# Attention layer: transposes of the score maxima moved from TensorE to VectorE, statistics and tail rearranged

## The reference

```python
B, T, D, H = 8, 512, 256, 16                    # head width 16
xn = layer_norm(x, norm_w, norm_b)
q = (xn @ q_w + q_b).reshape(B, T, H, 16)
k = (xn @ k_w + k_b).reshape(B, T, H, 16)
att = einsum('bnhl,bmhl->bnmh', q, k) + (1 - mask) * -1e6
att = softmax(att, axis=2)                      # over the keys m
v = ((xn @ v_w + v_b) * mask).reshape(B, T, H, 16)
y = einsum('bnmh,bmhl->bnhl', att, v).reshape(B, T, D)
e = silu(emb) @ emb_w + emb_b                   # emb is (8, 512)
scale, shift = split(e, 2)
h = layer_norm(y, sb_norm_w, sb_norm_b) * (1 + scale) + shift
out = x + silu(h) @ out_w + out_b
```

## Time and profile before

| | us |
|---|---|
| three runs | 513.33, 514.04, 513.12 |
| median | 513.33 |
| profiled execution | 512.97 |
| its span, first to last instruction | 511.2 |
| mean granted clock of TensorE | 1.00 |
| busy: TensorE, VectorE, ScalarE, POOL | 498.2, 408.1, 355.1, 232.3 |

### The profile page before, as it was taken

One profiled execution on the slowest core, in us unless ns is written; L12 is line 12 of the kernel. 1 busy time (PEld: TensorE's weight loads), 2 busy tenths in 40 slices (PEclk: granted clock), 3 DMA queues, 4 the chain that ended last, 5 costly groups with the idle time before them and its releaser, 6 DMA issues.

```text
span 511.2 us, 10072 instructions
## 1 busy us (share of the span) xinstructions
PE 498.2 (97%) x2829; PEld 188.8 (37%) x2829; DVE 408.1 (80%) x656; ACT 355.1 (69%) x647; POOL 232.3 (45%) x279
## 2 busy tenths in 40 slices
PE   8999999999999999999999999999999999999887
PEld 3433333343334333333334333343434343332225
DVE  7898778796888879797897978888788877879614
ACT  2336777678767778676867788677777778667872
POOL 5764333554354534635434643536346444333701
PEclk9999999999999999999999999999999999999999
DMA  5445452343423543334433443235433342234002
GB/s 153 134 138 158 121 167 93 105 126 111 126 74 109 151 144 105 100 90 144 123 89 120 146 132 108 76 100 154 135 104 115 92 142 82 87 110 144 0 2 83
DMA packets 54586, 57.42 MB, mean 112 GB/s; under 512 B 12424, under 2 KB 41736, under 8 KB 54560
## 3 DMA queue, kind: packets, MB, share of 16 engines
q1 hardware_dynamic: 51808, 54.74, 36.4%
q10 hardware_dynamic: 2752, 2.37, 1.6%
HBM read 35.82 MB, written 21.00 MB: 111 GB/s over the span
## 4 chain that ended last, share of the span: by engine, by line
PE 85%; DVE 7%; issue 3%; ACT 2%; POOL 1%; DMA 1%; POOLq 0%; ACTq 0%; DVEq 0%
PE pv_ps L625 24%; PE st_ps L609 22%; PE mx_ps L557 13%; PE job_ps L693 10%; PE job_ps L702 5%; DVE negmax L1092 4%; PE job_ps L714 3%; PE mx_ps L742 2%; ACT probs L858 2%; PE mx_ps L589 2%; PE mx_ps L668 1%; PE mx_ps L750 1%; DVE x_stats L1096 1%; DMA k_rows<-qk_dram 1%; PE job_ps L519 0%
## 5 line engine op out<-in xcount | busy, mean ns | idle before, releaser
L1092 DVE TENSOR_REDUCE negmax<-mx_ps 128x2 f32<-128x1024 f32 x256 | 304.8, 1220 | 76.3 <-PE mx_ps L557 75.9
L858 ACT ACTIVATE probs<-st_ps 128x512 f32<-128x512 f32 x502 | 272.4, 596 | 110.3 <-PE st_ps L609 105.8
L609 PE MATMUL st_ps<-q_rows,k_rows 115*128 115x512 bf16 x498 | 154.2, 383 | 2.4 <-ACT probs L858 0.9
L625 PE MATMUL pv_ps<-probs,v_rows 128*32 128x512 f32 x1024 | 136.4, 605 | 0.6 <-ACT probs L858 0.6
L1369 POOL TENSOR_TENSOR qk_parts<-qk_rest,qk_parts 128x512 bf16<-128x512 f32 x31 | 35.9, 1159 | 132.2 <-DVE qk_parts L1170 131.4
L557 PE MATMUL mx_ps<-k_rows,q_rows 51*128 51x512 bf16 x512 | 79.8, 382 | 1.8 <-DMA k_rows<-qk_dram 0.7
L609 PEld LDWEIGHTS st_ps<-q_rows,k_rows 115*128 115x128 bf16 x498 | 38.9, 97 | 106.3 <-ACT probs L858 75.4
L1354 POOL TENSOR_TENSOR qk_parts<-qk_full,zero 128x512 bf16<-128x512 f32 x29 | 30.1, 1039 | 72.1 <-ACT qk_full L888 72.1
L693 PE MATMUL job_ps<-x_norm_t,w_qk 128*128 128x512 f32 x116 | 59.6, 594 | 0.0
L557 PEld LDWEIGHTS mx_ps<-k_rows,q_rows 51*128 51x128 bf16 x512 | 16.3, 94 | 107.0 <-DVE negmax L1092 51.6
L1360 POOL TENSOR_TENSOR qk_rest<-qk_full,qk_parts 128x512 f32<-128x512 f32 x31 | 35.8, 1156 | 3.5 <-ACT qk_parts L876 1.2
(11 more groups left out here) (151 smaller groups left out, 401.0 us busy)
## 6 DMA issues: line engine op xcount, KB each, us to landing
qk_dram<-qk_parts SPq DMA_DIRECT2D x128, 128.0 KB
q_rows<-qk_dram SPq DMA_DIRECT2D x124, 96.0 KB, 2.6
k_rows<-qk_dram SPq DMA_DIRECT2D x124, 96.0 KB, 2.6
x_in<-in_x SPq DMA_DIRECT2D x16, 256.0 KB, 3.0
x_res<-in_x SPq DMA_DIRECT2D x7, 512.0 KB, 4.6
out<-out_sb SPq DMA_DIRECT2D x14, 256.0 KB, 2.5
k_rows<-mask_dram SPq DMA_DIRECT2D x64, 6.0 KB
w_e<-in_L_cond_emb_w ACTq DMA_DIRECT2D x4, 256.0 KB, 3.3
```

Of the source, the lines that this page charges most:

```text
L609: pe.matmul(st_bank(b, t, h), k_rows[0:ROWS_ALL, g, h, c * P:(c + 1) * P], q_rows[0:ROWS_ALL, g, h, :], start=True, stop=True).then_inc(st ...
L625: mm = pe.matmul(pv_ps[VW * h:VW * (h + 1), :], v_rows[:, c, g * GH + h, :], probs[:, t % P_SLOTS, h, :], start=(c == 0), stop=(c == CH - ...
L858: act.activation(probs[:, t % P_SLOTS, h, :], st_bank(b, t, h), ACT.Exp).then_inc(exp_done, 1)
L1092: dve.tensor_reduce(by_pair[:, :, j, c], mx_ps[j][:, :, :], AXIS_X, ALU.max, negate=True).then_inc(max_done, 1)
```

## The change

The turn of a group's maxima runs on VectorE, as four transposes of 32x32 blocks from `negmax` (padded to 32 columns) into a new tile `neg_rows`, ahead of reduction 0; the split reads `neg_rows` and stands behind reduction 0. Three turns stay on TensorE with the old order of the split: (0,0), (1,0) and (3,7). For the other 29, TensorE no longer waits for the split. The statistics of x go from t = 11 to 15 to t = 7 and 8, and `load_x` on SyncE from behind `spread(b, 0, 1)` to ahead of it. In the tail the last turn of y, its copy, moments, root and norms go by halves, `late_out` stands behind the turn of y but for one matmul, and the warming matmuls go.

```diff
+BLOCK = 32
-X_STAT = {(11, 0): (0,), (11, 2): (1,), (12, 2): (2,), (13, 1): (3,), (15, 0): (4,)}
+X_STAT = {(7, 2): (0, 1, 2), (8, 0): (3,), (8, 2): (4,)}
-WARM_LAST = 6
+def turn_on_pe(b, step):
+    turn = turn_at(b, step)
+    return turn is not None and isinstance(turn[1], int) and turn in ((0, 0), (1, 0), (NG - 1, B - 1))
-        negmax = sb("negmax", [P, 2, GH * CH])
+        negmax = sb("negmax", [P, 2, BLOCK])
+        neg_rows = sb("neg_rows", [BLOCK, P])
 # TensorE
             def max_pair(b, t, j):
+                if j == 1 and turn_on_pe(b, t):
+                    pe.wait_ge(max_split, turn_at(b, t)[0] + 1)
-                if j == 1 and turn_at(b, t):
-                    turn, turn_b = turn_at(b, t)
-                    pe.wait_ge(max_split, NG * turn_b + turn + 1)
             def max_turn(b, t):
-                if not turn_at(b, t):
+                if not turn_at(b, t) or not turn_on_pe(b, t):
                     return
+            def late_out(i, c, features):
...
+            def last_yturn():
+                pe.wait_ge(h_ready, KD * (B - 1))
+                pe.wait_ge(y_ready, NG * B - 1)
+                late_out(0, 0, range(1))
+                pe.wait_ge(max_done, PAIRS * STEPS * B)
+                for half in range(2):
+                    pe.wait_ge(last_yt, half + 1)
+                    for c in range(2 * half, 2 * half + 2):
+                        mm = pe.transpose(last_ps[0][half][:, c * P:(c + 1) * P], y_t[:, c * P:(c + 1) * P], ident[:, :])
+                    mm.then_inc(last_y, 1)
+                late_out(0, 0, range(1, KD))
+                late_out(0, 1, range(KD)).then_inc(turned["outp"], 1)
+                late_out(1, 0, range(KD))
+                late_out(1, 1, range(KD)).then_inc(turned["outp"], 1)
             def last_rows():
-                keep_warm(st_ps[0], WARM_LAST)
...
-                    if not short(b, t):
-                        max_turn(b, t)
 # ScalarE
+                if isinstance(b, int) and (b, g) == (B - 1, NG - 1):
+                    for half in range(2):
+                        tok = slice(2 * P * half, 2 * P * (half + 1))
+                        act.copy(y_t[:, tok], pv_ps[:, tok]).then_inc(last_yt, 1)
+                    return
                 act.copy(y_t[:, :], pv_ps[:, :]).then_inc(yt_ready, 1)
 # VectorE
             dve.memset(warm_in[:, :].bitcast(F32), 0.0).then_inc(warm_ready, 1)
+            dve.memset(negmax[:, :, GH * CH:], 0.0).then_inc(pad_ready, 1)
+            def turn_max(b, t):
+                if not turn_at(b, t) or turn_on_pe(b, t):
+                    return
+                i, d = turn_at(b, t)
+                n = NG * d + i
+                if isinstance(d, int) and n == 2:
+                    dve.wait_ge(pad_ready, 1)
+                dve.wait_ge(max_done, PAIRS * CH * (n + 1))
+                dve.wait_ge(max_split, n)
+                for c in range(CH):
+                    dve.transpose(neg_rows[:, BLOCK * c:BLOCK * (c + 1)], negmax[BLOCK * c:BLOCK * (c + 1), i % 2, :]
+                                  ).then_inc(turned["cturn"], 1)
-            def split_max(b, t):
+            def split_max(b, t, place):
+                if not turn_at(b, t) or place != (0 if turn_on_pe(b, t) else 1):
+                    return
...
-                dve.tensor_copy(parts[0], ps).then_inc(split_chain, 1)
+                dve.tensor_copy(parts[0], rows).then_inc(split_chain, 1)
                 dve.wait_ge(split_chain, n + 1)
-                dve.tensor_tensor(parts[1], ps, parts[0], ALU.subtract).then_inc(max_split, 1)
+                dve.tensor_tensor(parts[1], rows, parts[0], ALU.subtract).then_inc(max_split, 1)
...
+            def last_half(half):
+                chunks = slice(2 * half, 2 * half + 2)
+                by_head = last_ps[0][half][:, :].rearrange("p (c h w) -> p c h w", h=GH, w=VW)[:, chunks]
+                dve.wait_ge(last_y, half + 1)
+                dve.reciprocal(y_recip[:, chunks, :], by_head[:, :, :, HD]).then_inc(recip_ready, 1)
...
             def last_rows():
+                last_half(0)
+                last_half(1)
                 dve.wait_ge(turned["hturn"], KD * (B - 1))
                 for half in range(2):
+                    last_norm_half(half)
+                    late_sum(half)
...
                     stats_at(b, t, 0)
-                    split_max(b, t)
+                    turn_max(b, t)
+                    split_max(b, t, 0)
                     max_pair(b, t, 0)
+                    split_max(b, t, 1)
                     late_job(b, t, 1)
                     stats_at(b, t, 1)
                     max_pair(b, t, 1)
 # POOL
             def last_norms():
                 for half in range(2):
+                    chunks, c = slice(2 * half, 2 * half + 2), 2 * half
+                    pool.wait_ge(y_stat_ready, B + half)
+                    pool.tensor_tensor(y_rstd[:, chunks], y_vareps[:, chunks], exponent[:, chunks], ALU.pow
+                                       ).then_inc(y_rstd_ready, 1)
+                    pool.wait_ge(y_rstd_ready, B + half)
                     pool.tensor_scalar(y_norm[:, c, :], y[:, c, :], y_negmean[:, c:c + 1], y_rstd[:, c:c + 1],
                                        ALU.add, ALU.mult).then_inc(last_norm[half], 1)
 # SyncE, body(b)
-                spread(b, 0, 1)
                 if exists(b + 2) and not (isinstance(b, int) and b == -1):
                     wait_apart(sp, maskp_ready, x_norm_ready, CH * (b + 2))
                     load_x(b + 2)
+                spread(b, 0, 1)
```

More of the change, by code:

```diff
@@ L562, in max_pair, with max_turn @@
                     keep_warm(pv_ps, WARM_MAX.get((step, j), 0))
+            def max_turn(b, t):
+                if not turn_at(b, t) or not turn_on_pe(b, t):
+                    return
+                i, d = turn_at(b, t)
+                pe.wait_ge(max_done, PAIRS * CH * (NG * d + i + 1))
+                pe.transpose(mx_ps[1][0:GH * CH, 0, 0:P], negmax[:, i % 2, 0:GH * CH], ident[:, :]
+                             ).then_inc(turned["cturn"], CH)
             def first_score(h):
@@ L627, in pv_step @@
                 mm.then_inc(pv_done, 1)
-            def late_out(i, halves):
-                if i == 0 and 0 in halves:
-                    pe.wait_ge(h_ready, KD * (B - 1))
-                    pe.wait_ge(y_ready, NG * (B - 1) + NG - 1)
-                for c in halves:
-                    tok = (2 * i + c) * P
-                    for k in range(KD):
-                        mm = pe.matmul(late_out_ps[i][:, c * D:(c + 1) * D], h_t[:, k, tok:tok + P], w_o[:, k, :],
-                                       start=(k == 0), stop=(k == KD - 1))
-                if 1 in halves:
-                    mm.then_inc(turned["outp"], 1)
+            def late_out(i, c, features):
+                tok = (2 * i + c) * P
+                for k in features:
+                    mm = pe.matmul(late_out_ps[i][:, c * D:(c + 1) * D], h_t[:, k, tok:tok + P], w_o[:, k, :],
+                                   start=(k == 0), stop=(k == KD - 1))
+                return mm
+            def last_yturn():
[12 more added lines that the diff above has]
+                late_out(1, 1, range(KD)).then_inc(turned["outp"], 1)
             def last_rows():
-                keep_warm(st_ps[0], WARM_LAST)
                 for half in range(2):
@@ L1211, in stats_at, with last_stats, last_norm_half @@
                         y_stat(b - 1, at)
[L1213 to L1216 removed]
+            def last_stats():
+                dve.wait_ge(y_ready, NG * B - 1)
                 for c in range(CH):
[L1218 removed]
+                    dve.bn_stats(y_last_stats[:, c, 0, :], y[:, c, 0:D - GC]).then_inc(y_bn, 1)
+            def last_half(half):
[3 more added lines that the diff above has]
+                dve.reciprocal(y_recip[:, chunks, :], by_head[:, :, :, HD]).then_inc(recip_ready, 1)
+                dve.wait_ge(recip_ready, NG * B + half)
+                dve.tensor_tensor(y[:, chunks, D - GC:D].rearrange("p c (h l) -> p c h l", l=HD), by_head[:, :, :, 0:HD],
+                                  y_recip[:, chunks, :].unsqueeze(3).broadcast_to((P, 2, GH, HD)), ALU.mult).then_inc(y_ready, 1)
+                dve.wait_ge(y_ready, NG * B + half)
+                done = 2 * CH * (B - 1) + CH + CH * half
+                for c in range(2 * half, 2 * half + 2):
+                    dve.bn_stats(y_last_stats[:, c, 1, :], y[:, c, D - GC:D]).then_inc(y_bn, 1)
+                dve.wait_ge(y_bn, done + 2)
+                dve.memset(spacer[:, :], 0.0)
+                for c in range(2 * half, 2 * half + 2):
+                    dve.bn_aggr(y_mv[:, c, :], y_last_stats[:, c, :, :].rearrange("p a s -> p (a s)")).then_inc(y_bn, 1)
+                dve.wait_ge(y_bn, done + CH)
+                dve.tensor_scalar(y_negmean[:, chunks], y_mv[:, chunks, 0], -1.0, None, ALU.mult)
```

(6 more changed lines are left out.)

56 lines of the change are left out of this document (16 added, 40 removed).

## The result

| | before | after |
|---|---|---|
| median, us | 513.29 (512.76 to 515.42, 6 runs) | 509.67 (508.61 to 511.83, 6 runs) |
| ratio to before, 95% interval | | 0.9928 (0.9900 to 0.9955) |
| profiled execution; its span | 512.97; 511.2 | 510.14; 508.4 |

The change gains 3.6 us; 8.4 were forecast, and 509.67 lies above the range (503.0 to 508.4). In what follows a "step" is again the time from one first value product to the next, and a "loss" is how much longer a step is than the same step before.

The account below looks back on a forecast made before the run. TensorE was taken as the bound, busy 58.95 of a middle batch's 59.27 us. Terms: 7.3 + 1.9 + 0.4 + 0.2 = 9.8 off, 1.4 back, so 8.4 off: 504.9 us, range 503.0 to 508.4.

Parts of the forecast that it names:

- Turns to VectorE: 29 of 32 turns of the maxima leave TensorE; 27 of them save 0.27 us each, 7.3 us off.
- the stall of t=13: TensorE's wait in the step from t=13, laid to x's statistics on VectorE; moving them removes 6 x 0.32 = 1.9 us.
- Four block transposes: VectorE, ahead of reduction 0: 0.20 us each without overlap, 0.8 in all, hidden with 0.1 to spare.
- Batch 7: Last batch: VectorE's fuller stretch loses 0.2 us, the wait and turn at t=6 go; 0.4 us off, between 0.2 and 0.6.
- Who waits for the split: SyncE sends the maxima later, but they land with 0.7 us free before the tightest score; 0.2 us back in all.
- its load now stands ahead of the spread of group 0 on SyncE, some 1 us more ahead of two saves that are not awaited: SyncE: the load of x moves earlier so x is there for its statistics; no loss was charged for it.
- Rival C: Maxima land after 3.0 us instead of 1.8 at t=6 and 14, TensorE waits at the first score: 509 us; chance 0.05.
- Split behind reduction 0: VectorE at t=6 and 14: reduction 1 ends at Q+3.62, 3.60 allowed (Q: max matmuls' start); 0.08 on 14 steps, 1.1 us back.
- its reduction 1 of t=4 would end some 0.5 later than now, where about 0.55 are free. Nothing.: VectorE at t=3 and 4, working without a gap behind the later split of t=2: no loss expected.
- x's statistics: VectorE: moved to t=7 and 8, where they fit; the wait at t=13 goes, 1.9 us off.
- Rival E: VectorE's split, now reading SBUF, waits for a POOL instruction on 14 steps, 8 us: about 513 us; chance 0.04.
- Tail: End of the kernel by halves: POOL's root and norm take 1.02 and 0.63 whatever half, only TensorE's order gains; 0.2 us off.

Follow-up runs that it names:

- experiment 2: Changed kernel with x's statistics and load both back as in the kernel before: 508.94 us; with only the statistics back, the load still moved: 511.29 us.
- experiment 1: Changed kernel with the load of x as SyncE's first issue in every batch: 509.94 us, ratio 0.9939 to the kernel before.
- experiment 3: Changed kernel with the load of x as SyncE's first issue from batch 1 on, batch 0 as changed: 507.51 us, ratio 0.9901 to the kernel before.
- Experiment 5: Changed kernel with the split of the maxima ahead of reduction 0 at every turn: 511.45 us, ratio 0.9970 to the kernel before.
- experiment 6: Changed kernel with the cast of part 1 made by POOL instead of VectorE, from the third projection on: 510.86 us, ratio 0.9953 to the kernel before.
- experiment 8: Changed kernel, load first from batch 1; t=6: split ahead of reduction 0, cast behind reduction 1; t=14: cast on POOL; batch 0's load and statistics as before: 504.63 us.
- experiment 7: Changed kernel with cast of part 1 on POOL, split ahead of reduction 0 at t=6 and 14, load first from batch 1, batch 0's load and statistics as before: 507.63 us.

## Why the prediction was wrong

**Right.** "Turns to VectorE", 27 x 0.27, and the stall of t=13: 8.9 measured on 26 of the steps, 9.2 forecast. "Four block transposes": 0.198 each, not overlapped (0.89 for four), hidden. "Batch 7": 0.4.

**The step that failed** is "Who waits for the split", together with "its load now stands ahead of the spread of group 0 on SyncE, some 1 us more ahead of two saves that are not awaited". I costed the moved load as queue time, and only for the two saves, not for the maxima behind them, and did not ask what its 512 KB do to the transfer behind it. It stands 0.7 us behind the load of x_res, and the maxima, which the split behind reduction 0 had made later as well, follow 3.8 us behind it and land up to 3.8 later; in batch 0 they are also issued 0.75 late. That is 2.7 us in the profiled execution, where the sum had 0: about half of the 5.5 us that it missed. The two runs of experiment 2 show the load as the cause: moved alone the loss is there, put back it is gone; experiments 1 and 3 show the same by moving it away. Experiment 5 shows that an earlier issue of the maxima cures most of it too. Rival C, at 0.05, had the mechanism right and its 509 came close to 509.67, but the price only by luck: it put 4 us on 14 scores, at t=6 and t=14, and 2.7 us were lost on three, all at t=6; the rest up to 509.67 has other causes. Its "Against" took the median of landings of before for a kernel that puts a load next to them.

**Mis-sized: "Split behind reduction 0".** Reduction 1 ended at Q+3.73, the far end of the bounds; I took the middle, 0.08. Two differences: the cast starts 1.26 behind the reduction (1.14 was assumed), and the loss is 0.13 to 0.21 on 14 steps: 2.3 us instead of 1.1. That it is this chain, experiment 6 shows at t=14 (1.16 to less than 0.01) and experiment 8 at both.

**Also wrong, in batch 1: "its reduction 1 of t=4 would end some 0.5 later than now, where about 0.55 are free. Nothing."** In that batch VectorE has no 0.55 to spare at t=4, and TensorE's max matmuls of t=5 wait for that reduction:

```profile
113.94 0.39 PE L565 MATMUL mx_ps<-k_rows,q_rows 51*128 51x512 bf16 x2 [0.30 <-DVE negmax L1114]
```

The step from t=5 took 0.19 more than before instead of 0.27 less. In experiments 5, 6 and 7, which take the split or the cast of part 1 out from between the reductions of t=2, it takes 0.11 to 0.12 less than before.

**Right in sum, wrong in cause: "x's statistics".** The 1.9 us at t=13 came from the turn leaving TensorE. The move of the statistics alone is worth 1.4, and the load that it needed earlier cost 2.7. Without both the median is 508.94 (experiment 2), 0.7 better; the intervals of the two overlap, so the times alone do not show that gain.

**Rival E** was given 0.04 for the changed kernel, rightly: all 29 subtractions took 0.28 there. The mechanism it names is real on this chip, as experiments 6 and 7 show. It costs the changed kernel a little in batch 1: `h_t` at t=11 starts 0.02 behind POOL's instruction for the value rows and takes 1.25 us, 0.68 before, and the step from t=12 loses 0.41:

```profile
137.63 1.25 DVE L1213 SCALAR_TENSOR_TENSOR h_t<-h_tanh,h_lin 128x512 f32<-128x512 f32 x1
```

```profile
137.61 0.73 POOL L1436 TENSOR_TENSOR v_biased<-v_plain,vb_row 128x256 f32<-128x256 f32 x1
```

The profiles of the other runs agree. Where `h_t` takes 1.24 to 1.26 the step loses 0.39 to 0.41 (batch 1 in experiments 1, 2, 3 and 8, batch 6 too in 1 and the first of 2); in batch 1 of experiments 5, 6 and 7, where it takes 0.68 to 0.86, the step loses 0.01 or less. The rest of the single steps (0.5) stays open; most of it, too, is gone in experiments 5 and 6.

**The start.** The first value product came at 38.4, before at 37.5. In the profiles of the ten experiments it lies between 37.3 and 38.3. Experiments 1 and 3, which have the changed kernel's start, are at 37.3, so most of the 0.9 is probably scatter between executions. It was not tried by itself.

**Tail**: 0.55 in the profiles instead of 0.2. "POOL takes 1.02 for the root and 0.63 for a norm, whatever half" was wrong for the root: on two columns it took 0.71 and 0.78. The measured times can't tell 0.55 us from nothing.

## What to carry to other kernels

When a load is moved, look at which small, awaited transfer is issued within some 4 us behind it. Cost its issue behind the load and its landing with the load in flight, not with the median of a quiet queue. When a stall has two parties (an instruction that is late and one that waits for it), removing either ends it: ask which of two edits does it, since the other may then cost more than it brings. And before work is given to POOL, or moved in time on VectorE, lay POOL's timeline beside VectorE's operations from SBUF: 0.28 us became 2.48.
